# D times u from diagonal matrices on TensorE, copied by ScalarE, in a conditioned attention and Mamba block

## What is computed

```
u = silu(conv(x_in))                                # (8, 1024, 1024)
x_dbl = einsum('bsd,ed->bse', u, x_proj_w)
dt_r, B, C = split(x_dbl, [64, 80])
dt = softplus(einsum('bsr,dr->bsd', dt_r, dt_proj_w) + dt_proj_b)
...                                                 # scan over the 1024 steps: h = h * exp(dt*A) + dt*u*B, y = C.h
y = ys + u * D_param                                # D_param: one number per channel (1024)
y = y * silu(z)
return einsum('bsd,ed->bse', y, out_proj_w)
```

## Time and profile before

| | us |
|---|---|
| median of 3 runs | 7325.14 (7324.45 to 7329.71) |
| profiled execution | 7318.66 |
| its span | 7317.1 |

### The profile page before, as it was taken

The page is one execution under the profiler, slowest core; times in us unless marked ns, Lnnn a source line. Parts: engine busy times, 40 slices in busy tenths (PEclk is TensorE's granted clock), DMA queues, the critical chain, the costliest instruction groups (busy, mean ns, idle before and its releaser), DMA issues.

```text
span 7317.1 us, 135980 instructions
## 1 busy us (share of the span) xinstructions
PE 6329.8 (87%) x43360; PEld 4061.0 (55%) x43360; DVE 5947.7 (81%) x7137; ACT 4700.3 (64%) x6673; POOL 3147.3 (43%) x1533
## 2 busy tenths in 40 slices
PE   6998799987989879989799888898799987999878
PEld 2664457644575546745467445664457644575544
DVE  0678988789887998869978799778988799887995
ACT  2665677566675666746767467665677566675664
POOL 0105771067601774019730388105771067601773
PEclk9999899998999989999899998999899998999989
DMA  3425783367823777238752387425783367823676
GB/s 143 142 76 163 180 202 108 104 161 169 235 59 132 162 173 202 71 129 183 181 164 82 133 204 182 128 75 164 179 203 107 106 161 169 234 59 132 163 173 176
DMA packets 432975, 1092.28 MB, mean 149 GB/s; under 512 B 50056, under 2 KB 50184, under 8 KB 428000
## 3 DMA queue, kind: packets, MB, share of 16 engines
q1 hardware_dynamic: 256672, 671.49, 28.0%
q0 software_dynamic: 157120, 378.04, 26.6%
q10 hardware_dynamic: 18432, 33.56, 1.3%
HBM read 564.39 MB, written 250.10 MB: 111 GB/s over the span
## 4 chain that ended last, share of the span: by engine, by line
PE 70%; issue 10%; DVE 8%; DMA 4%; ACT 3%; POOL 3%; DVEq 1%; SPq 1%; ACTq 0%; POOLq 0%
PE ps L1233 43%; PE ps L1486 11%; PE ps L1334 9%; PE ps L1283 3%; POOL area_s L675 3%; DMA z_keep<-z_st 2%; DVE area_h L1156 2%; DVE area_s L1041 1%; PE ps L1285 1%; ACT k_stack L778 1%; DVE area_dt L1144 1%; PE ps L1435 1%; DMA k_stack<-qk_keep 1%; DMA area_acc<-area_w 1%; DVE area_u L1050 1%
## 5 line engine op out<-in xcount | busy, mean ns | idle before, releaser
L675 POOL TENSOR_TENSOR area_s<-area_u,area_s 128x1024 f32<-128x1024 f32 x1024 | 2537.0, 2547 | 667.3 <-DVE area_u L1147 385.0
L1156 DVE TENSOR_TENSOR_SCAN area_h<-ps,area_s 128x1024 f32<-128x1024 f32 x1024 | 2333.9, 2279 | 32.8 <-POOL area_s L675 19.1
L1486 PEld LDWEIGHTS ps<-ident,area_h 128*128 128x128 f32 x8192 | 1009.8, 151 | 960.8 <-DVE area_acc L1166 480.2
L1486 PE MATMUL ps<-ident,area_h 128*128 128x128 f32 x8192 | 1201.9, 294 | 383.3 <-DVE area_h L1156 205.7
L802 ACT ACTIVATE area_s<-area_s,negmax 128x1024 f32<-128x1024 f32 x1024 | 1177.3, 1150 | 519.8 <-DVE negmax L1041 517.4
L1041 DVE CUSTOM_DVE_ANT_0 area_s<-ps,area_dt 128x1024 f32<-128x1024 f32 x1024 | 1241.5, 1215 | 169.5 <-PE ps L1233 118.3
L662 POOL TENSOR_TENSOR area_s<-area_s 128x1024 f32<-128x1024 f32 x64 | 176.3, 2754 | 2651.8 <-ACT area_s L847 2651.8
L874 ACT ACTIVATE ps<-area_dt,negA 128x1024 f32<-128x1024 f32 x1024 | 1145.9, 1120 | 236.7 <-DVE area_h L1156 119.7
L860 ACT ACTIVATE area_w<-ps,C_nat 128x512 f32<-128x512 f32 x1024 | 704.4, 688 | 827.7 <-PE ps L1486 814.1
L1334 PE MATMUL ps<-ident,area_s 128*128 128x128 f32 x8192 | 1091.0, 277 | 16.6 <-ACT area_s L802 16.6
L1334 PEld LDWEIGHTS ps<-ident,area_s 128*128 128x128 f32 x8192 | 973.1, 143 | 168.7 <-issue 24.7
(11 more groups left out here) (125 smaller groups left out, 5598.8 us busy)
## 6 DMA issues: line engine op xcount, KB each, us to landing
area_acc<-area_w POOLq DMA_DIRECT2D x256, 1024.0 KB, 8.7
area_s<-b_rows SPq DMA_DIRECT2D x256, 512.0 KB, 5.1
q_stack<-qk_keep SPq DMA_DIRECT2D x520, 128.0 KB, 2.6
k_stack<-qk_keep SPq DMA_DIRECT2D x520, 128.0 KB, 3.2
qk_keep<-q_stack SPq DMA_DIRECT2D x144, 256.0 KB, 4.7
qk_keep<-k_stack SPq DMA_DIRECT2D x144, 256.0 KB, 5.2
area_s<-z_keep SPq DMA_DIRECT2D x72, 512.0 KB, 4.4
y_keep<-area_acc POOLq DMA_DIRECT2D x8, 4096.0 KB, 14.6
```

The source lines that it names most:

```text
L675: pool.tensor_tensor(dbu[:, dl % 2, :], U[:, k // (NS * DL) * DL + dl, :], bb[:, q, :], ALU.mult).then_inc(s_dbu.sem, 1)
L1156: v.tensor_tensor_scan(out=hs[:, q, dl, :], data0=banks(2 * (dl % 2)), data1=dbu[:, dl % 2, :], initial=0.0, op0=ALU.mult, op1=ALU.add).th ...
L1486: last = nc.tensor.transpose(ps[:, 4 + n % 2, dl * P:(dl + 1) * P], hs[:, r % 2, dl, n * P:(n + 1) * P], ident[:, :])
```

## The change

The transposes become products with a diagonal: stationary is the tile of U, as before, and moving is `D_diag[:, k, :]`, a 128 x 128 matrix with D of channel tile k on its diagonal, in place of the identity. What lands in PSUM is u * D, turned. ScalarE copies it into `acc` and signals `s_ai`; VectorE's product is gone. GpSimd makes the eight diagonals in each item, at the place of `D_bc`, from the identity and `D_col` (D by columns, 128 x 8), which one DMA in the prologue loads. The broadcast of D in each item is gone. ScalarE's copies stand ahead of and between the first two exponentials. TensorE waits once per item for the diagonals.

```diff
-        D_bc = area_h[:, 6 * T:7 * T]
+        D_diag = area_h[:, 6 * T:7 * T].rearrange("p (k c) -> p k c", k=ND)
...
+            sp.dma_start(D_col[:, :], D_row.rearrange("(k p) -> p k", p=P), allow_slow_non_contiguous=True).then_inc(s_dc.sem, 16)
...
-                sp.dma_start(D_bc, D_row.partition_broadcast(P)).then_inc(s_xpd.sem, 16)
...
+                pool.wait_ge(*s_av.at(b, G * HG * 2))
+                pool.nop(nofuse=True)
+                for k in range(ND):
+                    pool.tensor_tensor(D_diag[:, k, :], ident[:, :], D_col[:, k:k + 1].to_broadcast([P, P]), ALU.mult
+                                       ).then_inc(s_dd.sem, 1)
...
+                    def start_acc(n):
+                        act.wait_ge(*s_ut.at(b, n + 1))
+                        act.nop(nofuse=True)
+                        nc.scalar.activation(acc[:, n, :], banks(4 + 2 * (n % 2)), ACT.Copy).then_inc(s_ai.sem, 1)
+
+                    if dg == 0:
+                        act.wait_ge(*s_x1s.at(b, 16))
+                        act.nop(nofuse=True)
+                        for n in range(3):
+                            start_acc(n)
                     for pair in (0, 2):
                         for dl in (pair, pair + 1):
                             act.wait_ge(*s_dm.at(b, dg * DL + dl + 1))
                             nc.scalar.activation(dtmp[:, dl, :], dtmp[:, dl, :], ACT.Exp).then_inc(s_de.sem, 1)
+                            if dg == 0 and pair == 0:
+                                for n in ((3, 4) if dl == 0 else (5, 6, 7)):
+                                    start_acc(n)
...
-                dve.wait_ge(*s_xpd.at(b, 32))
-                dve.wait_ge(*s_x1s.at(b, 16))
-                for n in range(NT):
-                    dve.wait_ge(*s_ut.at(b, n + 1))
-                    v.tensor_tensor(acc[:, n, :], banks(4 + 2 * (n % 2)), D_bc[:, :], ALU.mult).then_inc(s_ai.sem, 1)
-                    if n == 1:
-                        dve.wait_ge(*s_ct.at(b, 1))
-                        v.tensor_copy(C_nat[:, :, :], banks(2).rearrange("p (n c) -> p n c", n=NT)[:, :, DTR + NS:XD]
-                                      ).then_inc(s_cn.sem, 1)
-                        clip(0)
-                    if n == 3:
-                        clip(1)
+                dve.wait_ge(*s_ct.at(b, 1))
+                v.tensor_copy(C_nat[:, :, :], banks(2).rearrange("p (n c) -> p n c", n=NT)[:, :, DTR + NS:XD]
+                              ).then_inc(s_cn.sem, 1)
+                clip(0)
+                clip(1)
...
+                pe.wait_ge(*s_dd.at(b, ND))
                 for n in range(NT):
                     if n >= 2:
                         pe.wait_ge(*s_ai.at(b, n - 1))
                     for k in range(ND):
-                        last = nc.tensor.transpose(ps[:, 4 + 2 * (n % 2) + k // 4, (k % 4) * P:(k % 4 + 1) * P],
-                                                   U[:, k, n * P:(n + 1) * P], ident[:, :])
+                        last = mm(ps[:, 4 + 2 * (n % 2) + k // 4, (k % 4) * P:(k % 4 + 1) * P],
+                                  U[:, k, n * P:(n + 1) * P], D_diag[:, k, :], 0, 0)
```

More of the change, by code:

```diff
@@ L255, in build @@
         warm = sb("warm", [P, 1])
+        D_col = sb("D_col", [P, ND])
         z_st = sb("z_st", [P, 512])
@@ L296, in build @@
         s_stk = [sig(f"qk_stacked{r}", 128 * G * HG // 2) for r in range(2)]
-        s_xpd = sig("wxp_D_loaded", 32)
+        s_xpd = sig("wxp_loaded", 16)
+        s_dc = sig("D_col_loaded", 0)
+        s_dd = sig("D_diag_ready", ND)
         s_wx = sig("wx_loaded", 16)
@@ L637, in _ @@
             pool.wait_ge(s_zk.sem, 16)
+            pool.wait_ge(s_dc.sem, 16)
             with pool.Fori(0, B) as b:
@@ L1396, in _ @@
                         pe.wait_ge(*s_c0.at(b, 5))
-                        pe.wait_ge(*s_xpd.at(b, 32))
+                        pe.wait_ge(*s_xpd.at(b, 16))
                     for th in range(TB):
```

## The result

| | median, us | range of the runs |
|---|---|---|
| before | 7324.8 | 7323.6 to 7329.7 |
| changed | 7371.5 | 7365.9 to 7374.0 |

The ratio is 1.0061 (95% interval 1.0044 to 1.0079), 46.7 us more. In us the interval is 32 to 58; where the time lies is read from the profiles. The forecast was 7365.6 with a range of 7346 to 7400. The profiled execution of the changed kernel took 7373.95 us, its span 7371.9.

The account below looks back on a forecast made before the run. It took TensorE to set the accumulator stage's pace up to 632.5 us, then VectorE; with the change TensorE throughout. Terms 35.4 - 4.4 + 8 + 1.5 = 40.5 us on the median 7325.14 gave 7365.6 us, range 7346 to 7400.

Parts of the forecast that it names:

- The main step: Accumulator stage: doubled tile time on TensorE alone sets the stage, P 4.42 us later per item, 35.4 us in all.
- P: Point in the accumulator stage where TensorE starts dt projections 2 and 3; clips 2 and 3, dt and scans follow.
- The relief of VectorE at zero: Accumulator stage: the 9.7 us per item (78 us in all) taken from VectorE counted as no gain.
- The clock comes back a little: The eight TensorE records at P: 3.70 us in every item, 4.4 us less in all.
- GpSimd's 8 us: End of attention: building diagonals on GpSimd holds up VectorE's four normalisations, 8 us in all, range 0 to 15.
- port conflict: End of attention: GpSimd and VectorE block one another; the forecast's low end, 7325 + 28, assumed none.
- The prologue's 1.5 us: Prologue: loading D by columns ahead of the embedding weights delays TensorE's first matmul, 1.5 us once, range 0 to 5.
- The load that shows: Rival, diagonal products: weight load not hidden, 0.140 to 0.190 us per record, 7397 to 7448 us, chance 0.13.
- the product at four transposes: Rival, diagonal products: four passes of 0.109 us per block, 3.5 us a tile, about 7478 us, chance 0.05.
- The product as cheap as a transpose: Rival, diagonal products: two records of 0.054 us, so TensorE runs as before and P hardly moves, 7329 us, chance 0.08.
- ScalarE as the bound of P: Rival, accumulator stage: ScalarE's copies set P at +14.5, 1.2 us earlier per item, 7311 us, chance 0.03.

Follow-up runs that it names:

- experiment 1: Changed kernel with the transposes of u back in place of the diagonal products, everything else as changed (D left out): 7350.3 us, ratio to before 1.0031.
- experiment 2: Changed kernel with the products, but VectorE instead of ScalarE copies the tiles out of PSUM: 7373.2 us, ratio 1.0069.
- experiment 3: Changed kernel with each diagonal product done twice into the same place: 7484.1 us, ratio 1.0220.
- experiment 8: Changed kernel with the faster reordering of clips, dt steps, exponentials and decays behind the dt projections: 7356.6 us, ratio 1.0045.
- experiment 6: Changed kernel with GpSimd building the diagonals later, once the second normalisation is turned: 7370.3 us.
- experiment 4: Kernel before, with useless transposes added in front of tile 0 in each item: 7370.8 us with 44, 7349.9 us with 22.
- experiment 7: Kernel before, VectorE's and ScalarE's order behind the dt projections changed: 7300.7 us; second kernel, with another order in the scan's second half: 7286.1 us.

## Why the prediction was right, and where it was not

**The main step held.** "So TensorE sets all of it": experiments 1 and 2 show it from both sides, and experiment 3 its price. The term was 4.42 us per item and measured 4.88, 39.0 us instead of 35.4. A record is 0.111 us and not 0.109, which is 0.26 us per item. The other 0.2 us lie in the handovers between the pieces: ScalarE starts the copy of the last tile 19.43 us behind the copy of xdT, which starts with the first tile to within 0.03 us, and I had +19.0. From there to P it is 1.08 us, as priced.

**The relief of VectorE at zero held.** It idles for 11.3 us ahead of clip 2. In experiment 8 its order no longer waits for P, and it idles as long, for ScalarE's logarithm. So the relief is worth nothing in the two orders that were run; for an order that has the logarithm earlier that isn't shown.

**"The clock comes back a little": right in kind, too large.** I took 4.4 us off, with 3.70 us at P everywhere. The two profiles of the changed kernel give 2.5 less and 1.6 more from P to the first dt than the first of before, so nothing on average. Over all thirteen profiles the kind is visible: with products ahead of P the records there were slowed in 7 of 48 items (4 of 16 in the changed kernel, none of 24 in experiments 2, 3 and 6, 3 of 8 in experiment 8), with transposes in 32 of 56 (8 of 16 in the kernel before, 7 of 8 in experiment 1, 8 of 16 in experiment 4, 9 of 16 in experiment 7).

What slows them is the moment at which the clock falls. It falls from 1.00 to 0.50 near P in each of these 104 items, with products too, from 0.1 us ahead of P to 7.8 us behind it. Where the records are slowed it comes before P + 2.8, and elsewhere after P + 4.4, when all eight are done. Two items, columns as in the earlier trace rows: item 0 of before, P at 639.64, and item 1 of the changed kernel, P at 1535.85:

```profile
639.64:641.68 2.04, 2.04 (x5) 1.04 (x6) 0.00 (x0) 0.99 (x1) 0.00 (x0) 1.00 0.36 138
641.68:644.86 3.18, 3.17 (x4) 0.67 (x2) 1.28 (x1) 1.06 (x1) 0.00 (x0) 0.50 1.04 387
```

```profile
1535.85:1539.55 3.70, 3.69 (x8) 1.41 (x8) 1.28 (x1) 3.67 (x4) 0.00 (x0) 1.00 0.67 251
1540.40:1545.00 4.60, 0.00 (x0) 0.00 (x0) 4.53 (x5) 3.29 (x5) 1.44 (x1) 0.50 0.61 213
```

I took 3.70 us everywhere because TensorE no longer idles up to the last copy. That puts the loss down to the gap of 1.31 us ahead of P, and it can't be all of it: the changed kernel still has one of 1.17 us, and experiment 1, with 1.18, lost the most. The transposes themselves ran at 1.00 there; only for the matmuls that follow them do the counts, 32 of 56 against 7 of 48, speak against transposes. But with transposes TensorE also idled between the tiles (0.45 and 1.23 us in item 0 of before), and with products it did not (busy for all of the 19.00 us from 627 to 646 in item 0 of the changed kernel); no run separates the two. Why the fall comes inside the eight records in some items and behind them in others of the same kernel stays open.

**GpSimd's 8 us were not there.** The term is mis-sized in two places: the length of a diagonal, 0.48 us by a line through two wider operations, where 0.40 was measured, and above all the guess that the normalisations would be held for a microsecond. In item 0 they lose 0.13 us and the small operations 0.3, which would be some 3 us in eight items. Experiment 6 can't tell even that from nothing. The forecast's range calls the term a port conflict; no run shows what the two engines would contend for, only these longer times.

**The prologue's 1.5 us were about 0.3.** TensorE's first matmul starts at 33.33 us instead of 33.20 in the first profiles, and at 33.19 instead of 32.58 in the second. Over all thirteen it is 33.19 on average with the load of D by columns and 32.89 without it. In the first 8 us the changed kernel moves 2,134 packets under 512 B instead of 1,104. So most of the 1,024 small pieces cost the matmul nothing.

**What I had not counted.** The mean of two profiles each is 6.7 us more in the normalisations and the start of the input projection, and 4.9 us more in scans and attention. The first is TensorE's clock, which is granted at 0.50 for 97.3 us of that stretch on average instead of 81.9. It comes as well in kernels that hold nothing of the change, with longer items (experiment 4) and with shorter ones (the first kernel of experiment 7, 445.1 us), so I take it for a matter of where the work falls in time and not of the change's parts; that is argued, not shown. Why the clock falls in one execution and not in another was not tried. Whether the 4.9 is the same, or GpSimd's share, stays open: with the old order behind P, the six profiles with diagonals lie at 5695.4 to 5703.9 there, and the four without them at 5692.2 to 5695.3. The terms too large and the terms left out nearly cancelled: 40.5 forecast, 46.7 measured. That the sum came closer than its parts is luck.

**The rivals.** The load that shows and the product at four transposes are excluded by experiment 3. The product as cheap as a transpose is excluded by the 16 records. ScalarE as the bound of P appears in experiment 1 only: there TensorE waits for ScalarE's copies, and P comes 15.2 us behind the first tile's start, where I had put these cases at 14.5 to 15.5.

## What to carry to other kernels

Before work is moved from one engine to another, ask which engine ends last in that stage, not which is busier over the span: 78 us of VectorE's work were taken away here, and VectorE only waited longer, because each fp32 transpose on TensorE became a product of two records (1.78 us a tile instead of 0.875). An engine's idle time ahead of a wait can be filled with what stands behind the wait: reordering clips and dt steps gave 38 us here with no work removed. And take a second profile before explaining 5 or 10 us in a stage that the change doesn't touch.

## What the runs showed of the hardware

- TensorE's granted clock fell from 1.00 to 0.50 near the same place in each of 104 items (13 profiles), but not at the same moment, and eight matmuls there took 3.70 to 7.19 us by it. Transposes ran at a granted clock of 1.00, and the fall came right behind them in seven of eight items of experiment 1. In item 0: 15 us in which the granted clock was 1.00 and TensorE busy for 12.8, then 7.19 us for the eight. The fall hit them in 32 of 56 items behind transposes and in 7 of 48 behind products.
- A true fp32 product of 128 by 128 by 128 is two records of 0.111 us, also in an unbroken row of 160 (18.13 us, 0.113 each), so that the weight load, 0.192 us on average, doesn't show even with so short a record.
- The same kernel's normalisations and start of the input projection differ by 3.7 and 2.5 us between two executions, summed over eight items, while the stretch from the first copy of the input projection to the copy of xdT, all of it with TensorE busy and a granted clock of 1.00 (before, item 0), repeats to 0.01 us (61.73 us in every item of every kernel).
